# Converting the edge records of a two-layer graph network in four VectorE instructions in place of ten

## The reference

```python
hs = h[src]
a = hs @ Ws.T + h[dst] @ Wd.T + emb_rel[etype] @ Wr.T
e = leaky_relu((a @ attn_fc2_w.T)[:, 0], 0.01)
w = exp(e - segment_max(e, dst)[dst])
alpha = w / segment_sum(w, dst)[dst]
x = layernorm(x + segment_sum(alpha[:, None] * hs, dst) + h @ loop_weight)
# then twice, h starting as x:
msg = (rel_embed[rel_id] + h[src]) @ W_r
h = rrelu(segment_sum(msg, dst) * deg ** -0.5 + self_msg)
```

## Time and profile before

| | |
|---|---|
| median of 3 runs | 2772.72 us (2772.16 to 2774.16) |
| the profiled execution | 2772.09 us |
| its span, first to last instruction | 2770.1 us |
| mean granted TensorE clock | 0.906 of full speed |
| busy: PE, DVE, ACT, POOL | 2148.2, 2044.5, 1222.7, 1590.8 us |

### The profile page before, as it was taken

How to read it: one execution, slowest core, us unless ns; L and a number is a source line. 1 busy time by engine, 2 the same in 40 slices (tenths; PEclk the granted TensorE clock), 3 DMA queues, 4 the chain that set the end, 5 groups by cost and what they waited for, 6 DMA issues and landing times.

```text
span 2770.1 us, 45483 instructions
## 1 busy us (share of the span) xinstructions
PE 2148.2 (78%) x16208; PEld 1803.9 (65%) x16208; DVE 2044.5 (74%) x4582; ACT 1222.7 (44%) x3215; POOL 1590.8 (57%) x1672
## 2 busy tenths in 40 slices
PE   1467666677677677787787788788787999999998
PEld 0355555566566566576676677667666876888887
DVE  6889998888888888898888888888887456333333
ACT  1265566555455555555555555555654323000000
POOL 6767777777777777777777777777774000000000
PEclk9888888888888888888889988999898999999999
DMA  8535554454554554554555555555444344666664
GB/s 222 164 117 166 174 172 141 149 176 146 157 181 145 157 182 150 154 184 152 166 176 157 169 175 164 172 169 174 154 153 153 108 157 135 215 209 212 215 211 158
DMA packets 184632, 463.50 MB, mean 167 GB/s; under 512 B 86336, under 2 KB 113784, under 8 KB 164577
## 3 DMA queue, kind: packets, MB, share of 16 engines
q1 hardware_dynamic: 116050, 339.10, 36.3%
q0 software_dynamic: 53600, 114.17, 15.8%
q10 hardware_dynamic: 14752, 7.26, 1.0%
HBM read 362.54 MB, written 97.84 MB: 166 GB/s over the span
## 4 chain that ended last, share of the span: by engine, by line
POOL 52%; PE 24%; issue 18%; DVE 4%; DMA 2%; ACT 0%; POOLq 0%; ACTq 0%; SPq 0%; DVEq 0%
POOL arena L568 52%; PE pair L960 19%; PE bank L884 1%; DVE arena L1124 1%; PE bank L845 1%; PE pair L933 1%; DMA wlp<-n_L_gnn_loop_weight_dram 1%; PE pair L963 1%; DMA group_starts<-endv 0%; DMA arena<-in_x_dram,srcw 0%; DVE arena L1101 0%; PE pair L814 0%; PE pair L791 0%; DVE arena L1071 0%; DVE arena L1072 0%
## 5 line engine op out<-in xcount | busy, mean ns | idle before, releaser
L568 POOL DMA_INDIRECT arena<-rows,srcw x1617 | 1540.4, 953 | 510.1 <-issue 492.2
L1124 DVE TENSOR_TENSOR arena<-bank,idx 128x2000 bf16<-128x2000 bf16 (+3 forms) x700 | 560.5, 853 | 22.4 <-PE pair L814 19.0
L960 PE MATMUL pair<-arena 125*125 125x384 bf16 x3285 | 551.4, 326 | 1.6 <-DVE arena L1325 1.6
L814 PE MATMUL pair<-arena 128*128 128x250 bf16 x2500 | 344.5, 285 | 262.2 <-DVE arena L1124 208.7
L590 ACT ACTIVATE arena<-pair 99x264 f32<-99x264 f32 (+2 forms) x410 | 278.8, 712 | 582.6 <-PE pair L814 448.9
L960 PEld LDWEIGHTS pair<-arena 125*125 125x125 bf16 x3285 | 447.4, 136 | 103.3 <-issue 8.4
L684 ACT ACTIVATE arena<-arena,wexp 128x128 f32<-128x128 bf16 x1650 | 487.4, 387 | 1.6
L884 PE MATMUL bank<-arena 128*125 128x130 f32 x3300 | 486.9, 319 | 0.0
L884 PEld LDWEIGHTS bank<-arena 128*125 128x125 f32 x3300 | 476.4, 230 | 3.9
L814 PEld LDWEIGHTS pair<-arena 128*128 128x128 bf16 x2500 | 237.8, 102 | 339.7 <-DVE arena L1124 271.5
L1101 DVE TENSOR_TENSOR arena<-arena,bank 128x4224 bf16<-128x4224 int16 x150 | 344.2, 2350 | 1.7
(11 more groups left out here) (250 smaller groups left out, 2311.5 us busy)
## 6 DMA issues: line engine op xcount, KB each, us to landing
arena<-counts SPq DMA_DIRECT2D x106, 812.5 KB, 4.4
counts<-arena SPq DMA_DIRECT2D x50, 1562.5 KB
arena<-dst SPq DMA_DIRECT2D x50, 1056.0 KB
arena<-etype SPq DMA_DIRECT2D x50, 1056.0 KB
arena<-rows,srcw POOLq DMA_INDIRECT x1617
arena<-counts SPq DMA_DIRECT2D x14, 281.2 KB, 2.7
edge_terms<-arena SPq DMA_DIRECT2D x200, 12.4 KB
xt<-in_x_dram SPq DMA_DIRECT2D x50, 62.5 KB
```

The source lines that it names most:

```text
L568: pool.indirect_dma_start(out=rows[:, q, c, :], out_offset=None, in_=rows0, in_offset=bass.IndirectOffsetOnAxis(ap=srcw[:, q, c:c + 1], ax ...
L814: r = pe.matmul(group_of(n, gi), ohl[:, sl, gi * GC + c, :], ohm[:, sl, gi * GC + c, :], start=(c == 0), stop=(c == GC - 1))
L960: r = pe.matmul(o, ring[0:TN, m % RD, h - h0, :], hs[k][0:TN, h, :], start=(h == first), stop=(h == last - 1))
L1124: return v.tensor_tensor(hot_.rearrange("p c (j t) -> p c j t", t=2), iotap[:, 0:w].rearrange("p (j t) -> p j t", t=2)[:, None, :, :].broa ...
```

## The change

The first instruction still makes i / 125 - 0.496. A value of 12582912 (1.5 times 2 to the 23rd) is then added and subtracted again in one instruction, which leaves the nearest whole number in float32. It takes the place of a cast to integer and back and of two corrections by one with their comparisons. Two scratch tiles go, and nothing else moves. The lines of the new kernel are 2 lower above the edit in `dve_fast`, and 8 lower below it.

```diff
+TO_WHOLE = 12582912.0
...
-        lo = carve([P, EW])
-        q_i = lo.bitcast(I32)
         qf = carve([P, EW])
-        off = carve([P, EW])
...
-                a, b, c, i_ = qf[0:EP], lo[0:EP], off[0:EP], srcl[0:EP]
+                a, i_ = qf[0:EP], srcl[0:EP]
                 link(v.tensor_scalar(a, i_, 1.0 / TN, -0.496, ALU.mult, ALU.add))
-                link(v.tensor_copy(q_i[0:EP], a))
-                link(v.tensor_copy(a, q_i[0:EP]))
-                link(v.scalar_tensor_tensor(b, a, -float(TN), i_, ALU.mult, ALU.add))
-                link(v.tensor_scalar(c, b, 0.0, None, ALU.is_lt))
-                link(v.tensor_tensor(a, a, c, ALU.subtract))
-                link(v.tensor_scalar(c, b, float(TN), None, ALU.is_ge))
-                link(v.tensor_tensor(a, a, c, ALU.add))
+                link(v.tensor_scalar(a, a, TO_WHOLE, TO_WHOLE, ALU.add, ALU.subtract))
                 v.scalar_tensor_tensor(recs[0:EP, :, GRAN:2 * GRAN], ...)
                 v.scalar_tensor_tensor(recs[0:EP, :, 0:GRAN], ...)
```

## The result

| | before | changed |
|---|---|---|
| median of 19 runs, us | 2773.56 (2769.97 to 2775.0) | 2768.82 (2766.14 to 2771.91) |
| span of the profiled execution, us | 2770.1 | 2766.6 |

The ratio is 0.9984, 95% interval [0.9978, 0.999]: 0.16% or 4.4 us faster, between 2.8 and 6.1 us. The forecast was 2766.9 us, 5.8 us faster, in a range of 2763.8 to 2769.6 us. The measured median lies in that range and 0.4 us above the forecast's own range of 2765.6 to 2768.4 us. The kernel before, which the forecast took at 2772.72 us from 3 runs, has 0.84 us more over 19.

What follows compares the result with a forecast made beforehand. POOL's gathers bound the run, all hanging on when tile 1's sum is done. 5.5 us from an earlier `terms(0)` plus 0.3 us of TensorE's clock make 2772.72 - 5.8 = 2766.9 us, range 2763.8 to 2769.6 us.

Steps and rivals of the forecast that it cites:

- The work removed: VectorE's records before `terms(0)`: seven instructions taking 9.70 us become one of 1.03 us, so VectorE is done 8.67 us earlier.
- The wait that takes over: In front of `terms(0)`: the load of `drw` becomes the wait, terms start at 102.12 us, gaining 5.5 us, not 8.67.
- The store behind the load: SP's queue: the 1.6 MB records store, issued right behind the `drw` load, should cost it some tenths of a us at most.
- Rival 2: Load of `drw` shares with the first quarter of the records store, losing 0.3 to 2 us: 2767.2 to 2768.9 us; 14%.
- Rival 3: Records store on the same queue holds `terms(0)` back to its end: terms at 108.1 us, run 2773.2 us; 3%.
- TensorE's clock: TensorE's sums of tiles 0 and 1: an earlier start meets the clock's rise sooner, +0.3 us, bound 0.9 us either way.
- The cover: Between 102 and 178 us: POOL, the gathered records and other waits have slack enough not to hold back the 5.5 us.
- Rival 1: Load of `drw` is there by 98.94 us, so all 8.67 + 0.3 us are gained: 2763.7 us; 5%.
- Rival 5: Something taken as covered sets the chain of tiles 0 and 1: 0 to 4 us left, 2768.7 to 2772.7 us; 5%.
- The rest of the run: From tile 3's gather to the end: the stretch stays 2770.1 - 178.1 = 2592.0 us within 1 us.
- one of the signs that I had named for a wrong forecast: Forecast wrong if `terms(0)` starts at 99 or after 103 us, a transfer wait appears before 172 us, or 2592.0 us shifts.
- moves all 47 later gathers by x: POOL never waits from 178.12 to about 2117 us, so moving tile 1's sum by x moves later gathers and last stage.

Runs made afterwards that it cites:

- before_again: The kernel before, unchanged, timed against itself and profiled anew on chips where every kernel ran far longer; ratio 1.0008 [0.9994, 1.0023].
- before_swap: The kernel before with two SP calls swapped, tile 0's edge terms stored and loaded before tile 1's wide lists are fetched; ratio 1.0 [0.9985, 1.0016] against the kernel before.

## Why the prediction was right, point by point

- **The work removed.** 8.67 us was right. From the first instruction of the records to the end of the last it is 5.62 us now and was 14.28 us, 8.66 us less.
- **The wait that takes over.** 5.5 us was forecast for the terms' start, with the load's arrival at 102.12 us; measured are 5.38 us and 102.23 us. The execution itself was 0.42 us late at the records and 0.25 us late at the load's issue. The estimate from the last packet and from another transfer's release gave 2.15 us behind the issue; the wait shows 2.01 us. The part taken from the other transfer, 0.55 us from the last packet to VectorE's start, was too long: here the last packet of 132 bytes ends 1.67 us behind the issue, which leaves 0.34 us.
- **The store behind the load.** Rivals 2 and 3 fall. The load took 2.01 us with the records issued 0.43 us behind it, and 1.88 to 2.04 us in all waits seen, with stores of 1.6 MB or the wide lists of 2.1 MB behind. The Trainium skill's up to 2 us for an access under high load (DMA: Bandwidth & Descriptors, section "Latency and other measured facts") would have added up to 1.8 us by the prediction's estimate; it did not show here, although the DMA engines moved 298 GB/s from 101 to 102 us. All nine waits have a large transfer behind the load, so the comparison is with the load's packets in the kernel before, which had nothing behind it for 7.8 us: their last one ended 1.62 us behind the issue, against 1.67 us now. The store cost the load 0.05 us at most. Rival 2's time did come: 2768.82 us lies in its 2767.2 to 2768.9 us. Its mechanism didn't, so the time alone would have named the wrong cause.
- **TensorE's clock.** The +0.3 us was nothing. The sum of tile 0 took 10.35 us, as before (10.37). The step that failed is "the clock rises at a moment of its own": it rose with the sum. The granted clock was again 0.50 in its first half, this row of the windows at 111 us being the one that answers to the earlier trace rows:

```profile
111.00:114.00 3.00, 3.00 (x16) 3.00 (x15) 3.00 (x2) 3.00 (x12) 2.17 (x3) 0.50 0.65 182
```

  The two rows below hold the rise from 0.50 to 1.00 (1.2 to 2.4 GHz). The first is of the kernel before, the second of the changed one. By their shares, 0.62 and 0.82, the rise came at 120.8 us before and at 115.4 us now, 5.8 and 5.7 us into the sum:

```profile
120.00:121.00 1.00, 1.00 (x7) 1.00 (x7) 1.00 (x2) 1.00 (x4) 0.69 (x2) 0.62 0.63 213
115.00:116.00 1.00, 1.00 (x9) 1.00 (x9) 1.00 (x1) 1.00 (x5) 0.69 (x2) 0.82 0.70 217
```

- **The cover.** What lay between the terms and tile 3's gather stayed off the path, as expected. POOL waited 10.16 us in front of tile 3's gather, the records' gather began at 108.93 us, and VectorE waits for no transfer between the terms and that gather. Rivals 1 and 5 are out: 5.4 us passed at the terms and 5.35 us at tile 3.
- **The rest of the run.** This is where the sum was off. I expected 2592.0 us within 1 us from tile 3's gather to the end and got 2766.6 - 172.77 = 2593.8 us, so one of the signs that I had named for a wrong forecast did come. The step that I had taken as exact, "moves all 47 later gathers by x", held up to tile 9 and then not between these two executions, whose gathers ran at a pitch 0.1% apart. Why the pitch differs stays open. Over 19 runs each the gain is 4.4 us with an interval of 2.8 to 6.1 us, which holds the 5.35 us. The forecast's place on the far side of 0.2% was wrong by about 1 us, and 0.3 us of that was the clock. The chances gave 50% to a gain above 0.2% and 47% to one within it; the second came. The range held, but a forecast 0.3 us beyond a line, with runs 5 us apart, was close to a coin toss on that line.

## What to carry to other kernels

Work in front of a wait is worth no more than the distance to the next thing that is waited for. Take it from the trace: the moment at which the transfer is usable (here 2.0 us after its issue), against the new end of the work. A wait that the trace of before doesn't show, because it is already over when the engine asks, is found in the code and dated by the transfer's last packets. A gain at the start of a long run of equal steps moves all of them if the limiting engine never waits in them. Here it was whole up to tile 9, and a difference of 0.1% in the pitch had taken 2.4 of 5.35 us by tile 49, so such a gain needs many runs to be seen.

## What the runs showed of the hardware

**A small load behind and before large ones.** The load of `drw` (49.5 KB in pieces of 132 bytes, DRAM to SBUF) was usable 1.88 to 2.04 us after its issue in nine waits, no matter that 1.6 to 2.1 MB were issued to the same queue 0.4 to 0.6 us later in all of them. What stands ahead of the stores of the terms costs more. With the wide lists ahead, the load was issued 100.22 - 91.16 = 9.1 us after the stores in the changed kernel and 126.66 - 118.53 = 8.1 us after them in before_again. With the wide lists moved behind, on the same chip (before_swap), it was 125.36 - 122.73 = 2.6 us.

**The gathers of POOL are slow while VectorE runs the records.** In the changed kernel four of POOL's gathers took 1.36 to 1.55 us against 0.94 us while the records ran, and the next, beyond them, 0.95 us. Before, seven took 1.41 to 2.59 us. It isn't only the instructions with two sources. Of the kernel before, the first row below ran beside the two casts, which have one source (94.44 to 96.46 us), the second beside the two writes of `recs`, which have two (104.14 to 107.70 us):

```profile
94.83 1.75 POOL L568 DMA_INDIRECT arena<-rows,srcw  x1 [0.30 <-issue]
105.22 1.56 POOL L568 DMA_INDIRECT arena<-rows,srcw  x1 [0.30 <-issue]
```

Beside the bfloat16 instructions just before the records (128 x 4224 and 128 x 6600, from 84.28 to 92.99 us) the gathers took 0.94 to 0.95 us. Both profiles at this pace show it. In the later groups the gathers of tile 1 were over before the records began, so no run tests which property of the instructions counts.

**Another pace in the later groups.** Chips 0, 2 and 13 had it; the record doesn't say on which chip the first measurement ran, so it can be the chip or the time. Where all kernels took some 4485 to 4540 us, TensorE had stretches with single instructions far apart, with nothing that the profile shows as a cause ("issue"). Of before_again:

```profile
272.49 0.33 PE L791 MATMUL pair<-arena 128*125 128x200 bf16 x1 [2.55 <-issue]
275.29 0.32 PE L791 MATMUL pair<-arena 128*125 128x200 bf16 x1 [2.47 <-issue]
277.39 0.32 PE L791 MATMUL pair<-arena 128*125 128x200 bf16 x1 [1.78 <-issue]
```

These starts are multiples of 0.70 us apart. Its windows, with and without gathers on POOL (columns as in the earlier trace rows):

```profile
250.00:285.00 35.00, 8.37 (x41) 6.41 (x41) 9.34 (x26) 4.61 (x5) 26.46 (x29) 0.59 0.39 115
291.00:314.00 23.00, 17.87 (x128) 14.71 (x129) 18.07 (x40) 16.77 (x50) 0.00 (x0) 0.79 0.21 78
```

TensorE ran 41 matmuls in 35 us while POOL gathered and 128 in 23 us while it didn't. The gathers themselves kept their pitch, and from tile 3 on POOL's wait for the sum of the tile before last became 29 us and more:

```profile
314.25 0.94 POOL L568 DMA_INDIRECT arena<-rows,srcw  x1 [29.02 <-PE bank L884]
```

So on these chips the other engines are slow while the gathers run, and POOL no longer sets the pace, since it waits in every tile. In the first profiles TensorE had no such gaps beside the same gathers: 11929 matmuls in 1939 us are 6.2 per us, against 1.2 and 5.6 in the two windows here. That the gathers are the cause is not shown. I have no experiment on it, and it stays open.
